# Head 0's score maxima made inside the stage of keys and values, and the keys' inverse scales turned there in four batches

## The reference, cut to what matters

```python
q = (x @ Wq + bq); kv = (cond @ Wkv + bkv)          # keys and values of 24,000 positions
q, k = _fq_sym(q * scale, axis=-1), _fq_sym(k, axis=-1)
v = _fq_sym(v, axis=2)
attn = softmax(einsum('bhqd,bhkd->bhqk', q, k))
attn = _fq_unsigned(attn, axis=-1)                   # its scale is max(attn) / 255 of each row
out = einsum('bhqk,bhkd->bhqd', attn, v) @ Wp + bp
```

## Time and profile before

| | us |
|---|---|
| median of 3 runs | 5092.93 (5092.11 to 5095.83) |
| the profiled execution, its own time | 5087.56 |
| its span, first to last instruction | 5086.3 |
| PE busy over the span | 4846.2 (95%) |
| DVE busy | 4129.8 (81%) |
| ACT busy | 3903.7 (77%) |
| POOL busy | 3523.8 (69%) |

### The profile page before, as it was taken

One profiled execution on the slowest core, in us unless ns is written; L12 is line 12 of the kernel. 1 busy time (PEld: TensorE's weight loads), 2 busy tenths in 40 slices (PEclk: granted clock), 3 DMA queues, 4 the chain that ended last, 5 costly groups with the idle time before them and its releaser, 6 DMA issues. The chain is left out here.

```text
span 5086.3 us, 167001 instructions
## 1 busy us (share of the span) xinstructions
PE 4846.2 (95%) x53945; PEld 2037.5 (40%) x53945; DVE 4129.8 (81%) x7118; ACT 3903.7 (77%) x6646; POOL 3523.8 (69%) x3679
## 2 busy tenths in 40 slices
PE   5999899999999999999999999999999999887979
PEld 3777622333333333333333333333333333324645
DVE  5767599989898988989898989989898989773242
ACT  1666502999999999999999999999999999981101
POOL 1555542888888888888888888888888888761000
PEclk8999855999999999999999999999999999998989
DMA  2666511111111111111111111111111111432000
GB/s 69 189 194 188 175 46 23 31 31 35 31 33 32 31 31 32 30 33 32 31 35 31 33 32 31 31 32 31 32 32 30 35 31 30 143 130 83 35 1 8
DMA packets 220749, 272.23 MB, mean 54 GB/s; under 512 B 34134, under 2 KB 199534, under 8 KB 219169
## 3 DMA queue, kind: packets, MB, share of 16 engines
q1 hardware_dynamic: 169153, 207.78, 14.7%
q10 hardware_dynamic: 50784, 53.76, 3.4%
HBM read 176.94 MB, written 82.97 MB: 51 GB/s over the span
## 5 line engine op out<-in xcount | busy, mean ns | idle before, releaser
L1186 ACT ACTIVATE e<-ps_sweep,sk 125x448 f32<-125x448 f32 x6144 | 3500.7, 633 | 209.5 <-ACTq L1185 105.5
L1234 DVE TENSOR_REDUCE unit_max<-ps_sweep 128x1 f32<-128x500 f32 x5376 | 3234.1, 670 | 281.6 <-DVEq L1233 262.0
L1454 POOL TENSOR_SCALAR r<-e 125x896 f32<-125x896 f32 x2976 | 2778.0, 949 | 601.9 <-POOLq L1453 539.8
L906 PE MATMUL ps_sweep<-q,k 54*128 54x448 bf16 x5760 | 1864.0, 354 | 8.0 <-ACT e L1186 1.0
L937 PE MATMUL ps_sweep<-k,q 48*128 48x500 bf16 x5376 | 1748.1, 390 | 38.7 <-PEq L936 31.0
L961 PE MATMUL ps_av<-e,zt 126*17 126x224 f32 x24576 | 1706.7, 353 | 0.0
L956 PE MATMUL ps_av<-r,vt 125*16 125x224 f16 x12288 | 852.6, 267 | 26.4 <-PEq L947 17.4
L937 PEld LDWEIGHTS ps_sweep<-k,q 48*128 48x128 bf16 x5376 | 350.6, 94 | 1233.7 <-issue 1228.0
L906 PEld LDWEIGHTS ps_sweep<-q,k 54*128 54x128 bf16 x5760 | 530.6, 93 | 519.5 <-issue 407.4
L961 PEld LDWEIGHTS ps_av<-e,zt 126*17 126x17 f32 x24576 | 627.1, 96 | 0.7 <-issue 0.2
L956 PEld LDWEIGHTS ps_av<-r,vt 125*16 125x16 f16 x12288 | 300.1, 85 | 714.9 <-issue 714.7
(11 more groups left out here) (236 smaller groups left out, 2705.8 us busy)
## 6 DMA issues: line engine op xcount, KB each, us to landing
k_rows<-krows ACTq DMA_DIRECT2D x48, 1000.0 KB, 8.8
k<-k_rows SPq DMA_DIRECT2D x408, 93.8 KB
k<-k_rows SPq DMA_DIRECT2D x128, 281.2 KB
cx<-in_ctxT SPq DMA_DIRECT2D x48, 500.0 KB, 5.0
v_raw<-vb SPq DMA_DIRECT2D x24, 1000.0 KB
vr<-v_raw SPq DMA_DIRECT2D x128, 187.5 KB
cb<-in_ctxT SPq DMA_DIRECT2D x16, 1500.0 KB, 6.2
gu_w<-in_gu SPq DMA_DIRECT2D x5, 1536.0 KB, 11.0
```

What stands on the lines that cost most here:

```text
L906: pe.matmul(score_bank(i, g, False)[:, 0:HALF], k2[u][:, i * KT:i * KT + P], q2[y][:, g * HALF:(g + 1) * HALF], start=True, stop=True, til ...
L1186: act.activation(e[i % SLOTS][0:KT, g, :], score_bank(i, g, both)[0:KT, 0:HALF], ACT.Exp, scale=sk[u][:, i:i + 1]).then_inc(e_wrote, 1)
L1234: top = dve.tensor_reduce(unit_max[:, b, j * NPIECE + at:j * NPIECE + at + 1], ps[:, 0:SB], axis=AX.X, op=ALU.max)
L1454: pool.tensor_scalar(r[i % SLOTS][:, :, :], e[i % SLOTS][0:KT, :, :], 1.0, HALFWORD, ALU.mult, ALU.add)\
```

## The change: what it does

In the stage of keys and values PE makes the scores of head 0 as well, from the turned keys that ACT has just copied (`rows`), against the queries of head 0 (`q0`, three copies loaded at the start). They lag the projection by four generations: 7 matmuls per generation, laid singly behind each projected tile and between the transposes. DVE takes their maxima at fixed places in its list. Two new PSUM banks hold the scores; the keys' banks fall from three to two. The key bank is now given back at the start of DVE's next step (`scaled_keys`), behind one maximum. `rows_kept` (ACT to PE) and `rows_used` (DVE to ACT) are new waits.

POOL splits the inverse scales per generation (`scale_parts`, 4 instructions over 125 x 64 numbers). Every 12 generations PE turns them in 18 transposes, ACT copies them in 3 and stores them with 6 transfers one generation later.

In the attention stage head 0's own first sweep is gone. DVE makes its final maximum and shift at once, the 9 early pieces of head 1 come first, the constants are put in another order on POOL, and PE waits for `ones_ready` and the rounded values in step 4 of head 0's second sweep.

```diff
-        psk = [psum(st, f"ps_k{i}", [KT, 2, DIM]) for i in range(3)]
+        q0 = sbuf(st, "q0", [HROWS, TOK], bf16)
+        t_parts = [sbuf(st, f"t_parts{u}", [KT, PARTS, HEADS, TBATCH], bf16) for u in range(2)]
+        psk = [psum(st, f"ps_k{i}", [KT, 2, DIM]) for i in range(2)]
+        ps1 = [psum(st, f"ps_first{i}", [QB, BANK]) for i in range(2)]
...
+            for i in range(PARTS):
+                sp.dma_start(q0[i * HDIM:(i + 1) * HDIM, :], q_rows[0:HDIM, :]).then_inc(q0_landed, 16)
...
+            def turn_scales(batch):
+                for r in range(PARTS):
+                    ps = pst[turned.next()]
                     pe.wait_ge(turn_free, 1).then_inc(turn_free, -1)
+                    flat = t_parts[batch % 2][:, r, :, :].rearrange("p h t -> p (h t)")
+                    for b in range(TB):
+                        last = pe.transpose(ps[:, b, 0:KT], flat[:, b::TB], ident_b[0:KT, 0:KT])
                     last.then_inc(rows_full, 1)
+            def pieces(n):
+                def piece(b):
+                    if not in_stage(n) or b >= NQB:
+                        return
+                    if b == 0:
+                        pe.wait_ge(rows_kept, 1).then_inc(rows_kept, -1)
+                    pe.wait_ge(s_free, 1).then_inc(s_free, -1)
+                    pe.matmul(ps1[(n * NQB + b) % 2][:, 0:GK], q0[:, b * QB:(b + 1) * QB],
+                              rows[n % 2][0:HROWS, DIM // P, :], start=True, stop=True, tile_position=(0, 0))\
+                      .then_inc(s_full, 1)
+                return piece
...
+            for n in range(NGEN + 4):
+                piece = pieces(n - 4)
                 for p in range(2):
+                    project(n, p, piece)
+                    turn(n - 3, 2 * p, piece)
+                if in_stage(n - 3) and batch_of(n - 3) is not None:
+                    turn_scales(batch_of(n - 3))
...
+            def scaled_keys(m):
+                dve.wait_ge(x_done, 1).then_inc(x_done, -1)
+                dve.sem_inc(k_free, 1)
+            def maximum(n, b):
+                dve.wait_ge(s_full, 1).then_inc(s_full, -1)
+                top = dve.tensor_reduce(unit_max[:, b, n:n + 1], ps1[(n * NQB + b) % 2][:, 0:GK], axis=AX.X, op=ALU.max)
...
             for m in range(2 * NGEN):
                 n, p = divmod(m, 2)
+                maximum(n - 4, 4 * p)
+                if m > 0:
+                    scaled_keys(m - 1)
+                maximum(n - 4, 4 * p + 1)
                 dve.wait_ge(k_full, 1).then_inc(k_full, -1)
...
                     quantised(m - 1)
+                maximum(n - 4, 4 * p + 2)
...
+                if p == 0:
+                    maximum(n - 4, 3)
...
+                scale_parts(n)
...
+                if in_stage(n - 3) and batch_of(n - 3) is not None:
+                    store_rows(n - 3)
+                    copy_scales(batch_of(n - 3))
```

In the attention stage (cut):

```diff
-            head(0, None, None, 0, True)
             head(1, 0, None, 1, True)
...
+                                if head_start and finished is None and i == LAG - 1:
+                                    pe.wait_ge(ones_ready, 1).then_inc(ones_ready, -1)
+                                    for half in range(2):
+                                        sum_values(u, half)
...
+            for n in range(sum(EARLY)):
+                piece(n, 1)
+            shift_rows((0,))
+            pe.wait_ge(pads_ready, 1).then_inc(pads_ready, -1)
             over_heads(head)
...
+            head_max(0)
+            high_part()
+            other_parts()
+            for n in range(sum(EARLY)):
+                piece(n, 1)
+            shift_rows(0, False)
+            value_scales()
...
-            scale_parts()
-            pool_done(pool.memset(zeros[:, :], 0.0))
```

More of the change, by code:

```diff
@@ L395, in pe_program, with project @@
         def pe_program():
-            def project(n, p):
+            def project(n, p, piece):
                 m, u = 2 * n + p, n % 3
[L399 to L403, removed]
-                for i in range(2):
[L405 to L412, removed]
@@ L414, in turn @@
-            def turn(n, lo):
-                if lo == 0:
+                if in_stage(n):
+                    if p == 0:
+                        pe.wait_ge(cx_ld[u], 16).then_inc(cx_ld[u], -16)
+                    pe.wait_ge(k_free, 1).then_inc(k_free, -1)
+                    pe.wait_ge(v_free, 1).then_inc(v_free, -1)
+                halves = ((psk[m % 2], 0), (psv[m % 2], DIM))
+                for i in range(2):
+                    if in_stage(n):
+                        tile = slice((2 * p + i) * KT, (2 * p + i + 1) * KT)
+                        for ps, lo in halves:
+                            pe.matmul(ps[:, i, :], ones[:, :], bias[:, lo:lo + DIM], start=True, stop=False)
+                        for c in range(NC):
+                            last = [pe.matmul(ps[:, i, :], cx[u][:, c, tile], wkv[:, c, lo:lo + DIM], start=False,
+                                              stop=(c == NC - 1)) for ps, lo in halves]
+                        if i == 1:
+                            last[0].then_inc(k_full, 1)
+                            last[1].then_inc(v_full, 1)
+                    piece(4 * p + i)
@@ L416, in turn @@
+            turned = Count()
+            def turn(n, lo, piece):
+                if in_stage(n) and lo == 0:
                     pe.wait_ge(low_ready, 1).then_inc(low_ready, -1)
                 for i in range(lo, lo + 2):
+                    if in_stage(n):
+                        ps = pst[turned.next()]
+                        pe.wait_ge(turn_free, 1).then_inc(turn_free, -1)
+                        for b in range(NBLK):
+                            last = pe.transpose(ps[:, b, 0:KT], parts[n % 4][:, i, b * P:(b + 1) * P],
+                                                ident_b[0:KT, 0:KT])
+                        last.then_inc(rows_full, 1)
+                    if i < GEN - 1:
+                        piece(2 * lo + 2 + i - lo)
@@ L551, in copy_rows @@
                     act.wait_ge(rows_out[u], 16).then_inc(rows_out[u], -16)
+                    act.wait_ge(rows_used, 1).then_inc(rows_used, -1)
                 act.wait_ge(rows_full, 1).then_inc(rows_full, -1)
-                copied = act.activation(rows[u][:, :, i * KT:(i + 1) * KT], pst[i % 2][:, :, 0:KT], ACT.Copy)
+                copied = act.activation(rows[u][:, :, i * KT:(i + 1) * KT], pst[copied_turns.next()][:, :, 0:KT], ACT.Copy)
                 copied.then_inc(rows_copied if i == GEN - 1 else turn_free, 1)
@@ L1413, in chunk @@
                             value_sums(1 - u, summed.index(i))
+                        if first and head_start and finished is None and i == LAG - 1:
+                            for half in range(2):
+                                value_sums(u, half)
                         for ahead, n in todo[-1:]:
@@ L1417, in chunk @@
                             shift_rows(y, not more)
-                        if not second and last and i == 0:
-                            value_scales()
                 over_chunks(chunk)
```

178 lines of the change are left out of this document (94 added, 84 removed).

## The result

The changed kernel takes 5059.19 us (median of 4 runs, 5056.7 to 5062.19) beside 5093.24 us for the kernel before on the same chip (4 runs, 5092.11 to 5095.83): ratio 0.9933, 95% interval 0.9915 to 0.995. The kernel is faster, by 34 us where 81 were forecast. The range held the time, the forecast of 5012 did not. The profiled execution is 5057.85 us.

A forecast was written before the change was run, and what follows sets the result against it. PE was taken to bound keys and values, DVE head 0's lone sweep. 5087.6 - 209.6 (start of attention) + 110 (44 generations) + 10 (batches) + 9 (end) = 5007, about 5012 us against the runs' median; range 4968 to 5064.

The forecast's parts named there:

- 209.6 us that were forecast for the start of attention: Attention's first instruction to head 0's clearing matmul: 235.6 us falls to 26, saving 209.6, bounds 203 to 212.
- the two things that were covered at nothing: Keys and values stage: two key banks instead of three, and `rows_kept` with 1 us of cover, each forecast to cost nothing.
- rival 2: Keys and values: small POOL instructions hold more of DVE, or `rows_kept` is late; generations 14 to 15 us, 5061 us; chance 0.18.
- the batches: Keys and values: three batches of inverse scales, PE waiting for ACT's copies, 3.5 us each, bounds 1 to 6, together 10.
- Rival 1: Keys and values: PE alone is the bound, generations of 12.4 to 12.8 us, 4978 us; chance 0.22.
- Rival 4: Keys and values: the maxima do not overlap, the stage grows by 198 us, 5100 us, no change; chance 0.02.
- PE alone would need 12.42 us: One generation of keys and values on PE: 10.88 us plus seven pieces of 0.22, 1.54 together.
- PE stands 0.8 us: Each generation of keys and values: PE waits 0.8 us for the fourth maximum's bank; generation 13.25, with gaps 13.4 us.
- The held L470: Keys and values: a maximum ahead of DVE's L470 makes it late, held until POOL's instruction ends, about 1.5 us every second step.
- rival 3: Keys and values: PE's clock falls at its stands; generations at half clock 22.8 us, 5153 us at 15 of them; chance 0.04.
- the end of the stage: End of keys and values: late transposes, copies, and issues with landing, 3 us each, +9, bounds 5 to 15.
- POOL's list at the start of attention: Start of attention to the clearing matmul: POOL's reordered instructions set the stretch, 26 us.

The follow-up runs named there:

- no_maxima: Changed kernel without DVE's 336 maxima of head 0 and PE's waits for their banks, a constant in their place: 5044.0 us, generations of 13.50.
- group_swap: swap_max with a generation's seven pieces grouped 1, 2, 2, 2 behind the four tiles, none between transposes: 5055.35 us, generations of 13.61.
- early_max: Changed kernel with DVE folding the previous generation's value maxima ahead of the rounding: 5053.27 us, ratio 0.992 to the kernel before.
- pool_probe: Changed kernel with a one-element POOL operation put behind the cross-partition maximum, before `zeros`: 5061.96 us.
- spread_split: Changed kernel with the three turns of scales one step apart and the six stores in two threes, one generation apart: 5055.78 us, ratio 0.9924.
- turns_first: Changed kernel with PE making a generation's turns ahead of its pieces once nothing is projected: 5057.31 us.
- combined_start: Changed kernel with early_max, grouped pieces, spread_split and turns_first, plus four fills of `e` moved to DVE and value scales ahead of the shift rows: 5040.29 us.
- swap_max: Changed kernel with the third and seventh score maximum of a generation moved behind the value maximum on DVE: 5069.59 us, generations of 13.81 to 13.82.
- spread_scales: Changed kernel with PE's three turns of scales spread half a generation apart, all six stores behind the last copy: 5090.92 us.

## Why the prediction was right and wrong

**Right.** The bound of both stages, and what folding one into the other takes away: 203.7 of the 209.6 us that were forecast for the start of attention are gone. Direction and range held. So did the two things that were covered at nothing and could have cost most, the two key banks and `rows_kept`: no row in the middle of the changed stage shows PE waiting for either. (At its beginning PE stands 0.57 and 0.25 us before tiles, for banks, and 1.32 us before the first piece.) At 13.75 us the generation is inside the forecast's own 13.0 to 13.9, so rival 2 did not come, though its 5061 us is nearest to the time: the measured 5059 has another make-up, a generation of 13.75 with the start, the batches and the end longer than forecast. Rival 1 (PE alone, 12.4 to 12.8 us) fell with `no_maxima`: PE alone is 13.5. Rival 4 fell with the generation's length.

**Wrong, the generation: "PE alone would need 12.42 us".** This is the step that failed first, and the largest line of the ledger (+16.1). I took a piece of 500 columns at 0.22 us, by the columns of the transposes. Its rows show 0.31 from start to start (400.08 to 400.39), 0.09 more. That is the price of one kind of matmul behind another, since the second piece of a pair takes 0.22 (`group_swap`); the forecast named such gaps and priced all of them together at 0.15 us (13.25 to 13.4). Cutting the 16 transposes in two groups costs 0.13 at each cut (0.55 for 8, 0.97 for 16), twice per generation, and the tile before a piece is 0.09 longer than before transposes. So 10.88 + 7 x 0.31 + 2 x 0.13 + 2 x 0.09 = 13.49, and `no_maxima` measured 13.50. **Wrong in the same sum, the other way: "PE stands 0.8 us".** A PE list longer by 1.1 us absorbs most of the stand; 0.26 was left. The two errors hid one another: 13.4 was forecast, 13.75 came, and its make-up was another one. The held L470 was right as a fact (1.57 us) and far too large as a cost. The stand that it leads to is 0.26 us, so it can cost no more than that; `early_max`, which is free of it, gains 0.1.

The Trainium skill (SBUF — State Buffer, "Who interferes with whom") says that a DVE instruction with two SBUF inputs contends with a GpSimd instruction that reads SBUF, and that a reduction never does. By that rule this hold was to be expected, and the trace agrees: L551, with two such inputs, 1.57 us beside L624, and the maxima (L528) 0.67 us at any place.

**Wrong, the batches: 3.5 us each, bounds 1 to 6.** At full clock the size was right: 3.6 in the second batch and 3.5 to 3.6 three times in `early_max`. What was missing is the clock. In the changed kernel it fell behind the first batch for part of a generation (windows show 0.66 in 280 to 285 us) and behind the third for 9.7 us, with PE's stands of 2.0 and 2.1 us ahead. With the same stands it did not fall behind the second batch of this very execution, nor in `early_max` (0.42, 0.50 and 1.09 us). In `pool_probe`, whose stage is the same code, it fell behind the second batch (0.61 in 450 to 460 us) and not behind the first. That is rival 3 at the place it named, at 1.5 and 4.8 us instead of 9 generations. What decides between a fall and none at such stands, these runs do not show. `spread_split` takes most of the cost away, by leaving PE no such wait in a row.

By the rule of the Trainium skill that the prediction cites (TensorE: Matmul & The Clock Gate, "A second HAM failure mode: psum-queue depth-cycling") the clock could swing all along the stage, since PE's pieces do cycle through two banks with a stand in each generation. It is 1.00 in 300 to 600 us, so this trace disagrees for one stand of 0.2 to 0.3 us in each 13.75.

**Wrong, the end of the stage: +9, bounds 5 to 15.** It is +20.1. The step that failed priced late turns, copies and issues, and took the 28 last maxima as running beside the rest. PE's list makes them part of the chain: pieces stand ahead of the turns and wait for DVE, 6.24 us at 756.86 while DVE does its last value maxima, then 1.67 and 0.56 us at the pairs; and a PE with such pauses is at 0.54 of its clock, so a generation of turns and pieces takes 9.6 us. `turns_first` returned 4 us. How the other 7 divide between waits and clock was not tried.

**Wrong, POOL's list at the start of attention: 26 us.** It took 31.9. The step that failed is the wait before the values. I read "143 idle <-issue" before L1462 as a wait and nothing else, and so missed 7.3 us of POOL's own which had lain inside it; the rest of the list came 1.4 us under its forecast. `pool_probe` shows the pause, and `combined_start` shows that this list still sets the start: four fills less, with the value scales made earlier, bring the clearing matmul 3.1 us forward.

**The first generations, +4.0.** The first 70 matmuls of the stage take 2.7 us longer in the changed kernel's profile, at a lower clock (before, then changed):
```profile
81.44:98.79 17.35, 17.35 (x70) 12.32 (x70) 6.44 (x15) 1.79 (x3) 0.00 (x1) 0.90 0.11 30
79.69:99.76 20.07, 20.07 (x70) 13.68 (x70) 6.38 (x15) 1.79 (x3) 0.00 (x1) 0.77 0.09 26
```
That is no cost of the change: with the same code there, `swap_max` takes 17.43 at 0.89 and `pool_probe` 21.79 at 0.70.

**Open.** From the clearing matmul to the end the changed kernel takes 8.3 us more than before (4230.3 beside 4222.0), and in the profiles of all twelve experiments it is 4228.6 to 4237.6. The clearing matmuls of head 0 and head 15 are 3501.0 us apart instead of 3498.3, and 2.4 of these 2.7 lie before the first sums (PE idle for 2.19 us), so they go with the changed start. The other 5.6 lie in the last 729.3 us (723.7 before), whose code the change does not touch. The twelve experiments show 724.1 to 732.2 there, and of the kernel before only one profile was kept, from an execution 5.4 us under the median; whether the 5.6 are more than such scatter is not shown.

## What to carry to other kernels

Count an interleaved matmul by the distance of starts where kinds alternate, not by its columns: seven small matmuls at 0.31 us, and two cuts through a row of transposes, made the list that bounded the stage. When one engine's idle room is filled with another stage's work, both may end near balance, as here (13.5 and 12.8 us), and then reordering rather moves a stand than removes it: five orders of the same work lay between 13.53 and 13.82 us. Look for short chains in a row (three waits for copies, six transfer issues on an engine that others wait for) and spread them: in `spread_split` PE's waits in a row went, and with them the falls of its clock.

## What was not expected of the hardware

- GpSimd pauses 7.3 to 8.4 us before its first two-operand operation behind a cross-partition maximum, also for a single element (7.25), and some 6 us before the maximum itself (5.87 to 6.45). Fills and the two `affine_select` in between don't pause. Before the change both pauses lay in time in which nobody waited for POOL, where they look like waiting.
- ScalarE's queue takes 0.55 to 0.7 us to issue each of six transfers beside a copy of its own (3.27 to 4.20 us for six), 0.95 to 1.1 in `spread_scales` (5.72 to 6.67), and 0.48 at the stage's end (2.85). All that stands behind them on that engine waits, signals too.
- PE's clock falls behind one row of stands that add up to about 2.1 us and not behind another in the same execution. A cost of this kind is not a constant of the code: a batch cost 3.6, 5.1 or 8.4 us.
- The clock also differs at the stage's beginning from one execution to the next: from PE's start to POOL's first L624 it took 17.3 to 22.0 us, at 0.90 to 0.69.
